# Attention on one core: the product with V in six visits instead of five, and unit 13's scores ahead of the last visit

## The chip, the cores and the metric

The kernel runs on one core of a Trainium2 chip. The metric is the device time of one execution in microseconds (us). Five engines work side by side, each through its own list of instructions: TensorE (PE; its weight loads are shown as PEld), VectorE (DVE), ScalarE (ACT), GpSimd (POOL) and SyncE (SP), which here only issues DMAs. An engine never passes over an instruction that waits for a semaphore, so what stands behind it waits too.

## What is computed

Input x is 4 sequences of 1024 tokens with 128 channels, all in float32. The reference adds an attention block and then a routed feed-forward block. Cut to what matters here:

```python
x = layernorm(layernorm(x)) * ln_w + ln_b            # 4 x 1024 x 128
q, k, v = x @ W_q + b_q, x @ W_k + b_k, x @ W_v + b_v   # 16 heads of 64
scores = q @ k.T / 8, causal mask, softmax
z = pattern @ v                                      # per head
x = resid + z @ W_o + b_o
# then: a mixture of 8 experts, 2 per token, layernorm, added to x
```

## The kernel before

Attention is done in 32 steps. A step is one pair of heads of one sequence, and has 16 **units**: unit n is query tile n // 2 (128 rows) of head n % 2, against its (n // 2 + 1) tiles of keys, so units grow from 128 to 1024 columns. Step 0, the last step and the loop body between them (30 passes on TensorE) come from one function per engine.

What a unit goes through, and under which names:

- TensorE, `scores(n)` (lines 722 and 723, full 128x128 array): two matmuls for each chunk of columns into `SPS[n % 2]`. It waits on `s_masked` until the mask of unit n - 2 has freed that buffer.
- VectorE, `mask(n)` (line 1082): masks, takes the row minimum into `NM` (a small second instruction reads it out) and writes `SSB[n % 2]`; then it signals `s_masked`.
- ScalarE, `act_exp(n)` (line 1380): the exponential into `PRS` (units 0 to 7) or `PRL` (units 8 to 15, a ring of four buffers), with the row sum.
- VectorE, `turn(n)` (line 1045): transposes the result in 32x32 blocks into `PTZ`. For even n it waits on `pv_done` until the step before has used up the key tile n // 2 there.
- TensorE, `values(...)` (lines 748 and 767): the product with V of **the step before** (`it - 1`). It runs with the array in tiles of 32 rows by 64 columns, one key tile after another; the sum over all eight is collected in the four PSUM banks `ZB`. One call is a **visit**: between visits stand scores, which use the whole array. The last two key tiles have their own order of matmuls (`last_values`) and signal once.

Behind the last visit comes the tail of the step before, `act_z` (line 1391): ScalarE copies Z out of `ZB` in two halves, banks 2 and 3 first, then 0 and 1. GpSimd's `divide` (line 532) scales by the row sums, TensorE's `out_of` (line 774) multiplies by W_o. `v_of` (line 712) projects V for the next step into banks 2 and 3 of `ZB`, so TensorE waits there for the first half of `act_z`:

```python
pe.wait_ge(z_copied, it * 2 - 1)
```

The last step has no `v_of`. After its scores TensorE also begins the next step: `scores(0, ahead=1)`, `out_of(1)`, then Q and K of the step after (line 706) between scores 1, 2, 3 and 4, and then the visit with key tile 0, which waits until unit 15 has been turned. On VectorE that turn stands directly behind `mask(2)`. The order is written out by hand in `pe_step`, `dve_step` and `act_step`; nothing schedules it at run time.

Of the kernel before, what the change touches and what calls it, by code (L numbers as in the profile page):

```python
# [55 lines left out]
def build_program(nc, a, out):  # L56
    with ExitStack() as ctx:
# [191 lines left out]
        def wait(eng, s, value):  # L249

            if not isinstance(value, int) or value > 0:
                eng.wait_ge(s, value)
# [25 lines left out]
        def spread_count(it):  # L278

            return (it + 1) * (SPREADS * DMA)  # L280

        def staged_count(it):

            return it * (3 * DMA) + 2 * DMA
# [501 lines left out]
        def pe_step(pe, it, first, last):  # L786

            step = it

            def scores(*units, ahead=0):  # L790
                it = step + ahead
                for n in units:
                    if not last and n in (UNITS // 2, UNITS // 2 + 1):

                        pe.wait_ge(qk_evac, it * 4 + n - UNITS // 2 + 7)
                    if n in (0, UNITS // 2):
                        c = n // (UNITS // 2)
                        pe.wait_ge(keys_spread[c], spread_count(it))
                        pe.wait_ge(q_split, it * 4 + 2 * c + 2)
                    wait(pe, s_masked, it * UNITS + n - 1)  # L800
                    pe_scores(pe, it, n)

            def qk(s):
                if last:
                    return
                if s == 0:
                    pe.wait_ge(staged, staged_count(it + 1))
                    if not first:
                        pe.wait_ge(x_staged[0], it * DMA)
                    pe.wait_ge(v_evac, it * 2 + 2)  # L810
                if s == 2:
                    if not first:
                        pe.wait_ge(x_staged[1], it * DMA)
                if s >= 2:

                    if first:
                        pe.wait_ge(s_masked, s - 1)
                    else:
                        pe.wait_ge(s_masked, it * UNITS + s - 3)
                pe_qk(pe, it + 1, s, ahead(s))  # L820

            def v_of(s):
                if last:
                    return
                if first:
                    pe.wait_ge(xt_ready, 6)
                else:
                    pe.wait_ge(z_copied, it * 2 - 1)
                    if s == 0:
                        pe.wait_ge(xv_staged, it * DMA)  # L830
                pe_v(pe, it + 1, s, ZB[:, 2 + s, :])

            def values(*blocks):
                if first:
                    return
                if blocks[0] == 0:
                    wait(pe, out_copied, it * 2 - 2)
                    if last:
                        pe.wait_ge(v_evac, it * 2 + 2)
                    else:  # L840
                        pe.wait_ge(qk_evac, it * 4 + 6)
                pe_values(pe, it - 1, *blocks)

            def out_of(g):
                if not first:
                    pe_out(pe, it - 1, g, TB[g])

            if first:
                scores(0, 1)
                qk(0)  # L850
                qk(1)
                scores(2)
                qk(2)
                qk(3)
                scores(3, 4)
            else:
                qk(0)
                qk(1)
                scores(1)
                qk(2)  # L860
                scores(2)
                qk(3)
                scores(3, 4)
            values(0, 1)
            scores(5, 6)
            if first:
                pe.wait_ge(qk_evac, 8)
                turn_norm(pe, 1)
            values(2)
            scores(7, 8)  # L870
            if first:
                turn_norm(pe, 2)
            values(3)
            scores(9, 10)
            if first:
                pe.wait_ge(xt_ready, 4)
                turn_norm(pe, 3)
            values(4, 5)
            scores(11, 12)
            values(6, 7)  # L880
            if first:
                pe_bias(pe)
            scores(13)
            v_of(0)
            v_of(1)
            scores(14)
            out_of(0)
            scores(15)
            if not last:
                scores(0, ahead=1)  # L890
            out_of(1)
# [230 lines left out]
        def dve_step(v, it, half, par, first, last):  # L1122

            def mask(n):
                dve_mask(v, it, par, n)

            def turn(*units):
                for n in units:
                    dve_turn(v, it, n, not first)

            def turn_back(n):
                if not first:
                    dve_turn(v, it - 1, n)

            def back():
                if not first:
                    dve_reciprocal(v, it - 1, 1 - par)

            if last:
                v.memset(BV[:, 0:P], 0.0).then_inc(zeroed, 1)  # L1140
                v.memset(ONES, 1.0).then_inc(zeroed, 1)
            if first:
                mask(0)
                mask(1)
                norm_late(v, 1)
            else:
                turn_back(13)
                mask(0)
            turn_back(14)
            if not first:  # L1150
                mask(1)
            mask(2)
            turn_back(15)
            back()
            mask(3)
            mask(4)
            if first:
                norm_late(v, 2)
            if last:
                v.wait_ge(out_evac, (STEPS - HP) * 2 + 1)  # L1160
                f_norm_stats(v, range(0, QT))
            if first:
                mask(5)
            turn(0, 1)
            if not first:
                mask(5)
            mask(6)
            turn(2, 3)
            mask(7)
            mask(8)  # L1170
            turn(4, 5)
            if last:
                f_norm_scale(v, 0)
            mask(9)
            mask(10)
            turn(6, 7, 8)
            mask(11)
            mask(12)
            if first:
                dve_bias(v)  # L1180
            turn(9, 10)
            mask(13)
            turn(11, 12)
            mask(14)
            mask(15)
# [213 lines left out]
        def act_step(act, it, half, par, first, last):  # L1399

            def exps_to(n0, n1):
                for n in range(n0, n1):
                    act_exp(act, it, par, n)

            def qk(s):
                if not last:
                    act_qk(act, it + 1, s, BQKS, ahead(s))

            def out_of(g):
                if not first:  # L1410
                    act_out(act, it - 1, g, TB[g])

            def v_of(s):
                if not last:
                    if s == 0:
                        act.wait_ge(v_stored[par], (half + 1) * DMA)
                    act_v(act, it + 1, s, ZB[:, 2 + s, :])

            if first:
                exps_to(0, 1)  # L1420
                qk(0)
                qk(1)
                exps_to(1, 2)
                qk(2)
                qk(3)
                exps_to(2, 7)
            else:
                act_exp(act, it - 1, 1 - par, UNITS - 1)
                qk(0)
                exps_to(0, 1)  # L1430
                qk(1)
                exps_to(1, 2)
                qk(2)
                qk(3)
                exps_to(2, 7)
            if first:
                norm_out(act, 1)
            if last:
                f_deviations(act, 0)
            exps_to(7, 9)  # L1440
            if first:
                norm_out(act, 2)
            exps_to(9, 11)
            if first:
                norm_out(act, 3)
            exps_to(11, 12)
            if not first:
                act_z(act, it - 1, 0)
                act_z(act, it - 1, 1)
            exps_to(12, 13)  # L1450
            v_of(0)
            exps_to(13, 14)
            v_of(1)
            out_of(0)
            exps_to(14, 15)
            out_of(1)
            if last:
                act_exp(act, it, par, UNITS - 1)
# [152 lines left out]
```

## Time and profile before

| | |
|---|---|
| median of 3 runs | 1099.04 us (1098.75 to 1099.82) |
| the profiled execution: time / span | 1098.83 us / 1097.1 us |
| PE busy, of the span | 1021.7 us, 93% |
| DVE, ACT, POOL busy | 862.3, 739.1, 740.1 us |
| instructions | 50146 |

The span runs from the first to the last instruction of one execution; its time has 1.73 us around it. "Busy" counts matmuls by modelled ends, so a TensorE that is busy 93% has few pauses, but is not at its peak rate. In the middle of the kernel every step looks like the one before it, so one step from visit to visit (500.12 us to 527.50 us) is read in detail, and the last step (from about 877 us to 909 us) beside it.

### The profile page before, as it was taken

To read this page: it belongs to the slowest core of one execution; us is meant where nothing else is said; L and a number is where in the kernel's file an instruction comes from. 1 tells how busy PE (TensorE), PEld (TensorE's weight loads), DVE (VectorE), ACT (ScalarE), POOL (GpSimd) and SP (SyncE) were. 2 spreads that over 40 slices of the span, in tenths; PEclk is the share of its full clock that TensorE was granted. 3 is DMA by queue.
4 is the path that set the end of the run, shared out by engine and by line. 5 is a ranking of instruction groups with operands and counts; after the bars stand their busy time and mean duration, and the time that the engine had idled before them with its cause. 6 is when DMAs were issued, how large, how long until landed. Compare 5 with 4: busy or idle time off the path is not lost.

```text
span 1097.1 us, 50146 instructions
## 1 busy us (share of the span) xinstructions
PE 1021.7 (93%) x19084; PEld 765.8 (70%) x19084; DVE 862.3 (79%) x2052; ACT 739.1 (67%) x1540; POOL 740.1 (67%) x725
## 2 busy tenths in 40 slices
PE   4799999999999999999999999999999988899986
PEld 2577777777777777777777777777777766454543
DVE  6878888888888888888888888888888876367574
ACT  3666666666666666666666666666666656667664
POOL 5797777777777777777777777777777734344644
PEclk8999999999999999999999999999999989999998
DMA  7678888778888788888888887888888863232422
GB/s 164 170 205 203 216 207 196 197 194 196 194 201 197 195 197 199 194 198 194 201 196 196 195 197 194 195 197 198 197 195 199 196 135 84 55 73 49 96 49 67
DMA packets 132766, 188.78 MB, mean 172 GB/s; under 512 B 46720, under 2 KB 60032, under 8 KB 132736
## 3 DMA queue, kind: packets, MB, share of 16 engines
q1 hardware_dynamic: 132736, 188.40, 71.6%
q8 instruction: 16, 0.26, 0.1%
q14 instruction: 14, 0.11, 0.0%
HBM read 133.39 MB, written 21.36 MB: 141 GB/s over the span
## 4 chain that ended last, share of the span: by engine, by line
PE 55%; DVE 27%; issue 14%; ACT 2%; DVEq 1%; DMA 1%; POOL 0%; SPq 0%; ACTq 0%
PE ZB L748 19%; DVE PTZ L1045 13%; PE SPS L722 9%; DVE SSB L1082 7%; PE SPS L723 6%; PE ZB L706 5%; PE ZB L774 3%; PE SPS L706 3%; PE SPS L939 1%; DVE NM L1082 1%; PE ZB L954 1%; PE SPS L913 1%; PE ZB L948 1%; PE ZB L931 1%; PE ZB L939 1%
## 5 line engine op out<-in xcount | busy, mean ns | idle before, releaser
L1082 DVE CUSTOM_DVE_ANT_0 SSB<-SPS,MASK 128x640 f32<-128x640 f32 (+7 forms) x512 | 375.6, 747 | 128.5 <-PE SPS L723 117.0
L722 PE MATMUL SPS<-KHP,QS 128*128 (+2 forms) x768 | 326.4, 431 | 20.1 <-DVE NM L1082 15.4
L1380 ACT ACTIVATE PRL<-SSB,NM 128x640 f32<-128x640 f32 (+3 forms) x256 | 253.4, 990 | 111.3 <-DVE NM L1082 107.7
L748 PE MATMUL ZB<-PTZ,VR 32*64 32x256 f32 (+3 forms) x12288 | 270.4, 308 | 16.0 <-DVE PTZ L1045 14.4
L748 PEld LDWEIGHTS ZB<-PTZ,VR 32*64 32x64 f32 x12288 | 229.2, 132 | 49.4 <-issue 38.3
L723 PE MATMUL SPS<-KLP,QS 128*128 (+2 forms) x768 | 261.3, 348 | 0.0
L1045 DVE STREAM_TRANSPOSE PTZ<-PRL 128x640 f32<-128x640 f32 (+3 forms) x256 | 257.7, 1027 | 0.0
L1380 ACT ACTIVATE PRS<-SSB,NM 128x128 f32<-128x128 f32 (+3 forms) x256 | 143.1, 559 | 137.6 <-DVE NM L1082 133.5
L722 PEld LDWEIGHTS SPS<-KHP,QS 128*128 128x128 f32 x768 | 145.6, 190 | 101.5 <-issue 69.7
L513 POOL TENSOR_TENSOR QS<-RAW,QS 64x512 fp32r<-64x512 f32 x128 | 165.2, 1290 | 10.3
L532 POOL TENSOR_TENSOR PTZ<-PTZ,RSB 128x512 f32<-128x512 f32 x64 | 81.1, 1288 | 133.2 <-ACT PTZ L1391 132.8
L723 PEld LDWEIGHTS SPS<-KLP,QS 128*128 128x128 f32 x768 | 145.9, 190 | 35.3 <-issue 22.6
L524 POOL TENSOR_TENSOR KLP<-RAW,KHP 64x512 fp32r<-64x512 f32 x126 | 162.1, 1286 | 10.1
L1045 DVE STREAM_TRANSPOSE PTZ<-PRS 128x128 f32<-128x128 f32 (+3 forms) x256 | 115.4, 489 | 16.9 <-PE ZB L748 16.9
L538 POOL TENSOR_TENSOR X<-X,OT 128x512 f32 (+1 forms) x64 | 81.8, 1278 | 63.6 <-ACT OT L1397 57.4
L511 POOL CAST QS<-RAW 64x512 fp32r<-64x512 f32 x128 | 77.5, 606 | 26.3 <-ACT RAW L1360 8.2
L522 POOL CAST KHP<-RAW 64x512 fp32r<-64x512 f32 x126 | 77.9, 618 | 13.2 <-POOL X L538 12.6
L774 PE MATMUL ZB<-WO,PTZ 128*128 (+1 forms) x512 | 67.4, 275 | 0.7 <-POOL PTZ L532 0.7
L774 PEld LDWEIGHTS ZB<-WO,PTZ 128*128 128x128 f32 x512 | 64.7, 191 | 4.0 <-POOL PTZ L532 1.1
L706 PE MATMUL SPS<-XTB,WQK 128*128 128x512 f32 x128 | 65.7, 598 | 0.0
L706 PE MATMUL ZB<-XTB,WQK 128*128 128x512 f32 x128 | 64.6, 630 | 0.1
L712 PE MATMUL ZB<-WV,XW 128*128 x480 | 61.1, 280 | 0.0
(178 smaller groups left out, 1209.6 us busy)
## 6 DMA issues: line engine op xcount, KB each, us to landing
VR<-v_scratch SPq DMA_DIRECT2D x248, 256.0 KB, 7.0
KHP<-KHP SPq DMA_DIRECT2D x64, 256.0 KB, 3.2
KLP<-KLP SPq DMA_DIRECT2D x64, 256.0 KB, 4.1
v_scratch<-V SPq DMA_DIRECT2D x32, 512.0 KB, 7.1
RSB<-rcp_scratch SPq DMA_DIRECT2D x64, 256.0 KB
XTB<-xt_scratch SPq DMA_DIRECT2D x62, 256.0 KB, 4.4
XW<-xt_scratch SPq DMA_DIRECT2D x30, 512.0 KB, 7.5
VR<-gate_scratch SPq DMA_DIRECT2D x16, 512.0 KB, 5.9
```

What stands on the lines that cost most here:

```text
L513: gp.tensor_tensor(QS[DH:P, h, part], q, high.bitcast(F32), ALU.subtract).then_inc(q_split, 1)
L524: gp.tensor_tensor(KL[par][DH:P, h, part], k, high.bitcast(F32), ALU.subtract).then_inc(k_split, 1)
L532: gp.tensor_tensor(z, z, RSB[:, g, :].rearrange("p (i t r) -> p i t r", t=TC, r=TR), ALU.mult).then_inc(zn_done, 1)
L538: gp.tensor_tensor(xs, xs, OT[:, :].rearrange("p (t d) -> p t d", d=D), ALU.add).then_inc(out_evac, 1)
L706: pe.matmul(bank, WQK[:, h, :], XTB[:, c * CH:(c + 1) * CH], start=True, stop=True).then_inc(qk_filled, 1)
L722: pe.matmul(SP_[n % 2][:, c0:c0 + wc], q, kh[:, c0:c0 + wc], start=True, stop=False)
L723: last = pe.matmul(SP_[n % 2][:, c0:c0 + wc], q, kl[:, c0:c0 + wc], start=False, stop=True)
L748: last = pe.matmul(ZB[h * DH:(h + 1) * DH, i, t0 * TR:QT * TR], VR[rows, j, kt, h * DH:(h + 1) * DH], turned_block(h, kt, j, rows, t0), st ...
L774: last = pe.matmul(bank[:, i * P:(i + 1) * P], ZN[g][:, i * P:(i + 1) * P], WO[:, bass.ds(it % HP, 1), :].rearrange("p o d -> p (o d)"), s ...
L1045: v.transpose(turned_of(n), exps_of(n)).then_inc(turned, 1)
L1082: v.tensor_tensor_reduce(out=SSB[n % 2][:, 0:w], in0=SP_[n % 2][:, 0:w], in1=MASK[:, S - w:S], scale=1.0, scalar=BIG, op0=ALU.add, op1=ALU ...
L1380: act.activation(exps_of(n), SSB[n % 2][:, 0:w], ACT.Exp, bias=NM[:, col:col + 1], scale=-1.0, accum_out=L[:, col:col + 1]).then_inc(exp_d ...
```

## The change

Three orders change, and nothing else: no instruction is added, removed or resized.

```diff
@@ pe_step
-            values(0, 1)
+            values(0)
             scores(5, 6)
-            values(2)
+            values(1)
             scores(7, 8)
-            values(3)
+            values(2)
             scores(9, 10)
+            values(3)
+            scores(11, 12)
             values(4, 5)
-            scores(11, 12)
-            values(6, 7)
             if first:
                 pe_bias(pe)
             scores(13)
+            values(6, 7)
             v_of(0)
             v_of(1)
@@ dve_step
-            turn(6, 7, 8)
+            turn(6, 7)
             mask(11)
             mask(12)
+            turn(8)
             turn(9, 10)
@@ act_step
-            exps_to(11, 12)
+            exps_to(11, 13)
             if not first:
                 act_z(act, it - 1, 0)
                 act_z(act, it - 1, 1)
-            exps_to(12, 13)
             v_of(0)
```

On TensorE, in the loop body, before: the end of the last visit (line 767), scores of unit 13, then `v_of` (line 712).

```order
L767 MATMUL ZB<-PTZ,VR 64x64 x2
L767 MATMUL ZB<-PTZ,VR 64x32 x24
L252 REGISTER_ALU
L722 MATMUL SPS<-KHP,QS 128x512
L723 MATMUL SPS<-KLP,QS 128x512
L722 MATMUL SPS<-KHP,QS 128x384
L723 MATMUL SPS<-KLP,QS 128x384
L828 REGISTER_ALU
L712 ISA
L712 MATMUL ZB<-WV,XW 128x128 x8
```

The same place after the change: the last of unit 13's scores, the last visit whole, then `v_of`.

```order
L723 MATMUL SPS<-KLP,QS 128x384
L767 MATMUL ZB<-PTZ,VR 64x64 x8
L767 MATMUL ZB<-PTZ,VR 64x32 x2
L767 MATMUL ZB<-PTZ,VR 64x64 x6
L767 MATMUL ZB<-PTZ,VR 64x32 x2
L767 MATMUL ZB<-PTZ,VR 64x64 x4
L767 MATMUL ZB<-PTZ,VR 64x32 x4
L767 MATMUL ZB<-PTZ,VR 64x64 x2
L767 MATMUL ZB<-PTZ,VR 64x32 x24
L828 REGISTER_ALU
L712 ISA
L712 MATMUL ZB<-WV,XW 128x128 x8
```

Nothing stands any more between the last matmul of the visit and `v_of`.

On TensorE, in the loop body, at the border of key tiles 0 and 1, before: key tile 0 ends with the 256-column matmuls, and key tile 1 (224 columns) follows at once.

```order
L748 MATMUL ZB<-PTZ,VR 64x224 x6
L748 MATMUL ZB<-PTZ,VR 64x256 x2
L748 MATMUL ZB<-PTZ,VR 64x224 x8
L748 MATMUL ZB<-PTZ,VR 64x192 x2
L748 MATMUL ZB<-PTZ,VR 64x224 x6
```

The same border after the change: the scores of units 5 and 6 stand in it.

```order
L748 MATMUL ZB<-PTZ,VR 64x224 x6
L748 MATMUL ZB<-PTZ,VR 64x256 x2
L252 REGISTER_ALU
L722 MATMUL SPS<-KHP,QS 128x384
L723 MATMUL SPS<-KLP,QS 128x384
L252 REGISTER_ALU
L722 MATMUL SPS<-KHP,QS 128x512
L723 MATMUL SPS<-KLP,QS 128x512
L748 MATMUL ZB<-PTZ,VR 64x224 x8
```

Every later pair of scores up to units 11 and 12 moves ahead of one key tile (or two) in the same way.

On ScalarE, around the copies of Z, before: exponential 11 (768 columns), the two copies, exponential 12 (896 columns).

```order
L1380 ACTIVATE PRL,L<-SSB,NM 128x768
L1390 ISA
L1391 ACTIVATE PTZ<-ZB 128x2x8x32 x2
L1377 REGISTER_ALU
L1380 ACTIVATE PRL,L<-SSB,NM 128x896
```

After the change (the same lines have numbers higher by two):

```order
L1382 ACTIVATE PRL,L<-SSB,NM 128x768
L1379 REGISTER_ALU
L1382 ACTIVATE PRL,L<-SSB,NM 128x896
L1392 ISA
L1393 ACTIVATE PTZ<-ZB 128x2x8x32 x2
```

Exponential 12 now stands ahead of the copies.

## Rows read from the trace of the kernel before

**Rows 1.** The page's chain of work that ended last, by engine

```profile
PE 55%; DVE 27%; issue 14%; ACT 2%; DVEq 1%; DMA 1%; POOL 0%; SPq 0%; ACTq 0%
```

**Rows 2.** Windows, steps 2 to 17: busy us, granted clock, DMA share, GB/s

```profile
55.00:493.00 438.00, 426.64 (x9205) 336.47 (x9206) 364.08 (x799) 303.30 (x671) 325.21 (x321) 1.00 0.82 199
```

**Rows 3.** Waits of PE, 600 to 870 us: total us, times, longest us

```profile
PE ZB L748 <- DVE PTZ L1045: 4.6, 10, 0.5
PE SPS L722 <- DVE NM L1082: 2.8, 10, 0.3
```

**Rows 4.** Timeline of PE, visits and first scores: start us, us, instruction

```profile
500.12 3.50 PE L748 MATMUL ZB<-PTZ,VR 32*64 32x256 f32 x128 [0.45 <-DVE PTZ L1045]
...
504.23 0.40 PE L723 MATMUL SPS<-KLP,QS 128*128 x1
504.56 1.56 PE L748 MATMUL ZB<-PTZ,VR 32*64 32x192 f32 x64
506.05 0.50 PE L722 MATMUL SPS<-KHP,QS 128*128 x1
506.38 0.39 PE L723 MATMUL SPS<-KLP,QS 128*128 x1
506.61 0.39 PE L722 MATMUL SPS<-KHP,QS 128*128 x1
...
507.40 1.37 PE L748 MATMUL ZB<-PTZ,VR 32*64 32x160 f32 x64
```

**Rows 5.** Timeline of PE, last visit to the next step's first visit

```profile
513.85 1.39 PE L767 MATMUL ZB<-PTZ,VR 32*64 32x64 f32 x104
515.17 0.50 PE L722 MATMUL SPS<-KHP,QS 128*128 x1
...
516.09 2.05 PE L712 MATMUL ZB<-WV,XW 128*128 x16
...
518.68 0.40 PE L723 MATMUL SPS<-KLP,QS 128*128 x1
...
520.49 0.40 PE L723 MATMUL SPS<-KLP,QS 128*128 x1
521.16 0.38 PE L722 MATMUL SPS<-KHP,QS 128*128 x1 [0.27 <-DVE NM L1082]
...
527.50 3.50 PE L748 MATMUL ZB<-PTZ,VR 32*64 32x256 f32 x128 [0.45 <-DVE PTZ L1045]
```

**Rows 6.** Timeline of DVE in the same step

```profile
506.95 0.69 DVE L1082 CUSTOM_DVE_ANT_0 SSB<-SPS,MASK 128x512 f32<-128x512 f32 x1 [0.75 <-PE SPS L723]
...
511.46 1.30 DVE L1045 STREAM_TRANSPOSE PTZ<-PRS 128x512 f32<-128x512 f32 x2
...
517.88 1.97 DVE L1045 STREAM_TRANSPOSE PTZ<-PRL 128x768 f32<-128x768 f32 x2
519.77 1.18 DVE L1082 CUSTOM_DVE_ANT_0 SSB<-SPS,MASK 128x1024 f32<-128x1024 f32 x1
520.89 0.08 DVE L1082 DVE_READ_ACCUMULATOR2_ANT NM<- 128x1 f32 x1
...
525.77 0.42 DVE L1082 CUSTOM_DVE_ANT_0 SSB<-SPS,MASK 128x256 f32<-128x256 f32 x1 [0.79 <-PE SPS L723]
526.12 1.24 DVE L1045 STREAM_TRANSPOSE PTZ<-PRL 128x1024 f32<-128x1024 f32 x1
```

**Rows 7.** Timeline of ACT: both copies of Z

```profile
515.31 1.06 ACT L1391 ACTIVATE PTZ<-ZB 128x512 f32<-128x512 f32 x2
```

**Rows 8.** Line 1391 over the kernel: ns min/median/max of one copy

```profile
L1391 ACT ACTIVATE PTZ<-ZB x64: 576/586/598, 77.2 to 928.5; 128x512 f32<-128x512 f32 x64
```

**Rows 9.** Timeline of POOL: both divisions

```profile
516.60 2.54 POOL L532 TENSOR_TENSOR PTZ<-PTZ,RSB 128x512 f32<-128x512 f32 x2 [3.87 <-ACT PTZ L1391]
```

**Rows 10.** Timeline of PE in the last step

```profile
882.88 6.36 PE L748 MATMUL ZB<-PTZ,VR 32*64 32x256 f32 x128 [0.67 <-DVE PTZ L1045]
...
905.79 1.16 PE L774 MATMUL ZB<-WO,PTZ 128*128 128x128 f32 x8 [0.70 <-POOL PTZ L532]
```

## The prediction

> **What bounds the kernel now.** I read the page first. It gives TensorE 93% of the span, but its chain of work puts 27% on VectorE [rows 1], so the two views don't name the same engine. The windows settle the shares: in the steady part TensorE is busy 426.64 of 438.00 us at a granted clock of 1.00 (the upper level, 2.4 GHz), VectorE 364.08 [rows 2]. The list of waits then tells what the remaining 2.6% is: per step TensorE pauses twice for VectorE, once for a transpose (ten times in ten steps, about 0.46 us) and once for a mask (ten times, 0.28 us) [rows 3]. The timeline of one step places them. The first visit of V begins at 500.12 and again at 527.50, so a step is 27.38 us [rows 4, 5]. One pause is before that visit; the other, at 521.16, is before `scores(0, ahead=1)` and ends with the mask of unit 14 (its minimum is read out by 520.97, TensorE goes on 0.19 later) [rows 5, 6]. There are no other pauses. So TensorE paces the step, VectorE catches it at two points, and a new order can gain at most those two pauses and must not open a third.
>
> Counted from start to start, the pause at 521.16 is larger than its 0.27: full chunks of scores follow each other by 0.23 (506.38 to 506.61) [rows 4], so after the one at 520.49 the next was due at 520.72 and came 0.44 late [rows 5].
>
> **The change, part by part.** All matmuls, masks, exponentials, transposes, copies and DMAs stay, in number and size. What can change is the price of switching between scores and visits, and who waits.
>
> *A sixth visit.* Key tile 2 alone takes 1.56 us and key tile 3 alone 1.37 [rows 4], 0.19 less for one tile of queries less. Continued upwards, key tiles 1 and 0 alone would take 1.75 and 1.94, together 3.69, against 3.50 in one visit [rows 4]. Each visit's last matmuls overlap the scores behind it by 0.07 (504.56 + 1.56 = 506.12, next start 506.05) [rows 4], so the split adds 3.69 - 3.50 - 0.07 = 0.12. The way in costs 0.10: from the last scores (504.23) to the visit (504.56) it is 0.33 where scores follow by 0.23. The way out costs 0.10 as well: 506.05 to 506.38 is 0.33 [rows 4]. The new sixth way out is the one from the last visit into `v_of`, behind the new wait, and its 0.10 is the price of weights loaded uncovered; the scores at 521.16, which now would not come out of a pause, save about the same (an estimate from the same 0.10). I let these two cancel. Visits: **+0.22 us a step**, bounds 0 (the extrapolation fails, and the way in hides) and 0.35.
>
> The Trainium skill, TensorEngine Tiling (Array Packing), Key Properties, says that changing the tiling mode makes the array drain. Visits and scores are in two such modes, and the change makes ten mode changes a step into twelve. The 0.33 against 0.23 agrees with it; were the rule without effect here, the time would come out about 7 us lower than mine.
>
> *The last visit directly ahead of `v_of`.* Today the last visit ends at 513.85 + 1.39 = 515.24 and ScalarE starts the copies 0.07 later, at 515.31; the first is done after 0.59, at 515.90, and `v_of` starts at 516.09 [rows 5, 7, 8]. In between TensorE does the scores of unit 13 (515.17 to 516.09, 0.92). They hide the copy almost exactly. After the change that cover is gone. `v_of` could start 0.07 before the visit's modelled end; instead it starts 0.07 + 0.59 + 0.14 to 0.19 behind it (0.14 is from the end of the transpose at 526.12 + 1.24 = 527.36 to 527.50, 0.19 the mask's release above) [rows 5, 6]. That is 0.87 to 0.92: **+0.89 us a step**. The bound from below is 0.70, if the second half's distance (1.06 - 0.59 = 0.47) is what a copy costs and ScalarE starts at once [rows 7]; the bound from above is 1.0. Behind the wait stand `v_of`, scores 14, `out_of(0)` and scores 15. Exponential 12 is ahead of the copies now, but it must not be late: VectorE's masks 11 and 12 come out earlier (below), and even with turn 8, whose buffer of the ring it needs, behind mask 12, it is over well before the visit's end. Leaving it behind the copies would have been harmless too.
>
> *Masks earlier.* The new starts on TensorE, with the pieces above (1.87 and 1.68 for key tiles 0 and 1 up to the next start, all other distances as today): scores 5 at 501.99, 7 at 504.68, 9 at 507.52, key tile 3 at 509.10 to 510.47, scores 11 at 510.40, scores 13 at 513.97, last visit 514.99 to 516.38. Scores 5 to 13 reach VectorE 1.2 to 1.8 us sooner. Transposes are held by key tiles instead: turn 6 needs key tile 3, free at 510.47, so about 510.6 instead of 511.46. From there to the end of turn 12 VectorE has the same instructions and today no pause, ending at 519.77 [rows 6]; so it is done at about 518.9. TensorE meanwhile is later by 0.22 + 0.89 (+0.10) = 1.21 from `v_of` on: scores 14 end at 519.08 + 1.21 = 520.29, and VectorE waits for them.
>
> *The pause for mask 14.* It arises today since mask 14 starts at 519.77, behind turn 12, though scores 14 end at 518.68 + 0.40 = 519.08 [rows 5, 6]. A free VectorE starts 0.17 after the scores (506.38 + 0.39 = 506.77, 506.95) [rows 4, 6]: at 519.25 in today's times. Mask and readout take 1.20 (519.77 to 520.97), the release 0.19: 520.64, and TensorE is due at 520.72. So the pause goes, with 0.08 to spare: **-0.44 us a step**; bounds -0.44 and 0.
>
> *The pause for turn 15.* Mask 2 starts as soon as scores 2 are there (VectorE idles 0.79 before it), turn 15 follows at 526.12 and the visit 0.14 behind its end [rows 5, 6]. All of it hangs on TensorE's own scores 2 and moves with them. Mask 15 is now released by scores 15 rather than by mask 14: VectorE gets later against TensorE by about 0.43 of the 0.79, and another 0.10 goes where scores 0 come out uncovered no more. 0.26 is left, so this pause stays as it is: 0.
>
> *Others.* The divisions start 0.23 after the copies' end (516.37 to 516.60) and take 1.27 each [rows 9]; new: about 517.7 to 519.0, and `out_of(0)` comes at about 520.1. Covered by 1.1 us. SyncE's spread of V waits for key tile 3, later by 1.7 us, and for the last visit; both feed a visit 15 us or more later. GpSimd's splits and its adds shift with the step.
>
> **The sum.** 0.22 + 0.89 - 0.44 = +0.67 us for each of the 30 steps with a `v_of` behind a visit, 20.1 us. The last step has no `v_of`, but its `out_of(0)` already waits 0.70 for GpSimd [rows 10], so the whole chain visit, copies, division shows: the visit ends later by 0.22 and by the scores 13 now ahead of it (0.92 + 0.10), about 1.2 us. Step 0 has no visits. Together +21.3 on the profiled execution's 1098.83 (1.73 around its span; the median of runs, 1099.04, is 0.02% off): **1120 us**, 1.9% slower. 0.2% is about what a measurement of this kernel can tell from no change, and this is far above it.
>
> **Rivals.**
> - *The mask 14 pause stays* (0.08 is little): something makes VectorE 0.5 late, say a turn held longer by a key tile. Then +1.11 a step, 33 + 1.2: 1133 us.
> - *Switching is free, or the copy's release shorter.* Without the 0.22 and with 0.75 for the wait: +0.31 a step: 1109 us.
> - *VectorE paces the step* (other side). For it: the 27%, and both pauses end there [rows 1, 3]. Then the earlier masks are worth their whole effect, the copy of Z falls into a time in which TensorE would wait anyway, and the step gains 0.44 - 0.22: 31 steps, -7 us: 1092 us. It decides once the wait before `v_of` is under 0.22 us. Against it: the copy alone takes 0.58 at least in all 64 cases [rows 8], and at that point TensorE has no pause today that could take it in.
> - *The clock falls.* In the last step, behind several pauses of TensorE, the first visit took 6.36 us instead of 3.50 [rows 4, 10]: the lower level, 1.2 GHz. Were each step's new pause to do that to one visit, 2.9 us a step would be added: about 1207 us. The Trainium skill, TensorE: Matmul & The Clock Gate, Part 1, has the clock fall after an idle engine; by it a longer pause would count. Against it: two pauses a step today, at a clock of 1.00 [rows 2, 3].
>
> **Chances.** The forecast with its bounds 0.78, the pause that stays 0.09, the cheap case 0.06, VectorE as the pace 0.03 (faster), the clock 0.02, and 0.02 for a balance near nothing. The range 1109 to 1134 takes in the first three. Faster by over 0.2%: 0.04; within: 0.03; slower: 0.93.
>
> **What would show it.** A new pause of some 0.8 us in every step, TensorE line 712 waiting for ScalarE's copy of Z, 30 times; no or nearly no wait of scores for a mask; the transpose pause still about 0.46; six visits, of about 1.94 and 1.75 us for the first two; steps of 28.05 us. VectorE's idle time should sit before mask 14 and before the turns of units 2, 4 and 6. I am wrong if the copy is released much faster than other hand-overs, if the pause at mask 14 survives, or if the visits' length hides stalls that the new order removes, which the modelled ends can't show.

## The result and the profile after

| | before | after |
|---|---|---|
| median of 4 runs each, same chip, us | 1099.23 (1098.75 to 1099.82) | 1121.27 (1120.95 to 1123.54) |
| ratio to before | | 1.0206 [1.0194, 1.0219] |
| profiled execution: time, span, us | 1098.83, 1097.1 | 1123.54, 1121.5 |
| granted clock in steps 2 to 17 | 1.00 [rows 2] | 1.00 |
| one step, first visit to first visit, us | 27.38 [rows 4, 5] | 28.09 |

The change costs 22.0 us, 2.1%; 1120 was predicted. The profiled execution of after is the longest of its four. In step 2 one of its visits waits 2.0 us for the spread of V, a wait that the trace of before doesn't have; whether the other three executions had it isn't known. The comparisons below go by a step of the steady part, which this doesn't touch.

The page of after: the span, the busy time of the engines, and the chain of work that ended last.

```profile
span 1121.5 us, 50146 instructions
...
PE 1026.5 (92%) x19084; PEld 758.9 (68%) x19084; DVE 869.7 (78%) x2052; ACT 741.3 (66%) x1540; POOL 740.1 (66%) x725
...
PE 79%; DVE 9%; ACT 4%; issue 3%; DMA 3%; SPq 1%; POOL 0%; DVEq 0%; POOLq 0%; ACTq 0%
```

The number of instructions is the same. VectorE's share of the chain fell from 27% [rows 1] to 9% and TensorE's rose from 55% to 79%, while the kernel became slower: a share of the chain tells whom the end is traced through, not what the step costs.

The waits of TensorE in the trace of after, from 600 to 880 us (total us, times, longest us).

```profile
PE ZB L712 <- ACT PTZ L1393: 8.3, 10, 0.8
PE ZB L748 <- DVE PTZ L1046: 4.6, 10, 0.5
```

Against [rows 3], the waits of scores for a mask are gone, the transpose pause stands as it was, and a new and larger wait has come: `v_of` for ScalarE's copy of Z, once a step. The same list over the whole kernel:

```profile
PE ZB L712 <- ACT PTZ L1393: 25.0, 30, 0.8
PE ZB L748 <- DVE PTZ L1046: 14.0, 30, 0.7
...
PE SPS L722 <- DVE NM L1083: 6.9, 8, 2.3
...
PE ZB L748 <- DMA VR<-v_scratch: 2.0, 1, 2.0
```

The new wait comes 30 times and sums to 25.0 us, more than the whole loss; before, the waits for a mask were 36 and 15.4 us over the whole kernel, so 28 of them and 8.5 us have gone. The last row is the wait in step 2. Now one step of TensorE after (start us, duration us), the answer to [rows 4, 5].

```profile
512.97 1.99 PE L748 MATMUL ZB<-PTZ,VR 32*64 32x256 f32 x64 [0.45 <-DVE PTZ L1046]
514.89 0.44 PE L722 MATMUL SPS<-KHP,QS 128*128 x1
...
515.57 0.40 PE L723 MATMUL SPS<-KLP,QS 128*128 x1
515.90 1.77 PE L748 MATMUL ZB<-PTZ,VR 32*64 32x224 f32 x64
517.60 0.50 PE L722 MATMUL SPS<-KHP,QS 128*128 x1
...
527.92 1.39 PE L767 MATMUL ZB<-PTZ,VR 32*64 32x64 f32 x104
530.14 2.05 PE L712 MATMUL ZB<-WV,XW 128*128 x16 [0.83 <-ACT PTZ L1393]
531.95 0.48 PE L722 MATMUL SPS<-KHP,QS 128*128 x1
...
534.77 0.34 PE L722 MATMUL SPS<-KHP,QS 128*128 x1
...
541.06 1.99 PE L748 MATMUL ZB<-PTZ,VR 32*64 32x256 f32 x64 [0.46 <-DVE PTZ L1046]
```

The reader is to see three things. Key tiles 0 and 1 are visits of 1.99 and 1.77 us with scores between. Behind the last visit TensorE stands for 0.83 us until `v_of` at 530.14. And from `v_of` to the next first visit it is 10.92 us, against 11.41 before (516.09 to 527.50 [rows 5]): there the mask's pause is missing. The other side of the new wait is ScalarE:

```profile
527.46 1.04 ACT L1382 ACTIVATE PRL<-SSB,NM 128x896 f32<-128x896 f32 x1 [0.80 <-DVE PTZ L1046]
...
529.35 1.08 ACT L1393 ACTIVATE PTZ<-ZB 128x512 f32<-128x512 f32 x2 [0.75 <-PE ZB L767]
```

Exponential 12 is over before the copies, with ScalarE idle for 0.75 us in between. The first copy starts 0.04 us behind the visit's modelled end (527.92 + 1.39 = 529.31), and takes 0.59. And VectorE in the same step:

```profile
515.01 0.51 DVE L1046 STREAM_TRANSPOSE PTZ<-PRS 128x128 f32<-128x128 f32 x2 [0.35 <-PE ZB L748]
...
517.72 0.77 DVE L1046 STREAM_TRANSPOSE PTZ<-PRS 128x256 f32<-128x256 f32 x2 [0.86 <-PE ZB L748]
...
520.56 1.04 DVE L1046 STREAM_TRANSPOSE PTZ<-PRS 128x384 f32<-128x384 f32 x2 [0.52 <-PE ZB L748]
...
529.86 1.97 DVE L1046 STREAM_TRANSPOSE PTZ<-PRL 128x768 f32<-128x768 f32 x2
533.30 1.22 DVE L1083 CUSTOM_DVE_ANT_0 SSB<-SPS,MASK 128x1024 f32<-128x1024 f32 x1 [1.47 <-PE SPS L723]
534.45 0.08 DVE L1083 DVE_READ_ACCUMULATOR2_ANT NM<- 128x1 f32 x1
...
539.34 0.42 DVE L1083 CUSTOM_DVE_ANT_0 SSB<-SPS,MASK 128x256 f32<-128x256 f32 x1 [0.43 <-PE SPS L723]
539.69 1.24 DVE L1046 STREAM_TRANSPOSE PTZ<-PRL 128x1024 f32<-128x1024 f32 x1
```

Mask 14 (533.30) now waits 1.47 us for its scores, where in [rows 6] it started late, behind a transpose. The transposes wait for key tiles instead, and 0.43 us is left ahead of mask 2 (0.79 before [rows 6]).

### The profile page after: what moved, and what is told of

Its sections match the earlier page's. It is cut to its first block, busy times and chain, and to the rows that moved or that the text cites. A ratio compares the mean times of both kernels' runs of the same rounds, so it can differ in the third digit from the quotient of the medians.

```text
span 1121.5 us, 50146 instructions
## 1 busy us (share of the span) xinstructions
PE 1026.5 (92%) x19084; PEld 758.9 (68%) x19084; DVE 869.7 (78%) x2052; ACT 741.3 (66%) x1540; POOL 740.1 (66%) x725
## 4 chain that ended last, share of the span: by engine, by line
PE 79%; DVE 9%; ACT 4%; issue 3%; DMA 3%; SPq 1%; POOL 0%; DVEq 0%; POOLq 0%; ACTq 0%
PE ZB L748 23%; PE SPS L722 14%; PE SPS L723 11%; PE ZB L712 5%; PE ZB L774 5%; PE ZB L706 5%; PE ZB L767 4%; DVE PTZ L1046 3%; PE SPS L706 2%; ACT PTZ L1393 2%; PE SPS L940 1%; PE ZB L955 1%; PE SPS L914 1%; PE ZB L949 1%; PE ZB L932 1%
## 5 line engine op out<-in xcount | busy, mean ns | idle before, releaser
L748 PE MATMUL ZB<-PTZ,VR 32*64 32x256 f32 (+3 forms) x12288 | 277.3, 307 | 16.3 <-DVE PTZ L1046 14.0
L748 PEld LDWEIGHTS ZB<-PTZ,VR 32*64 32x64 f32 x12288 | 220.9, 131 | 58.0 <-issue 45.0
L712 PEld LDWEIGHTS ZB<-WV,XW 128*128 128x128 f32 x480 | 55.8, 191 | 28.2 <-issue 28.2
```

The costliest lines, as they stand in the source:

```text
L712: last = pe.matmul(bank[:, k * P:(k + 1) * P], xt[:, t * P:(t + 1) * P], WV[:, bass.ds((it % HP) * 2, 2), :].rearrange("p h e -> p (h e)") ...
L748: last = pe.matmul(ZB[h * DH:(h + 1) * DH, i, t0 * TR:QT * TR], VR[rows, j, kt, h * DH:(h + 1) * DH], turned_block(h, kt, j, rows, t0), st ...
```

## The experiments

The theory is that of the prediction: the step grows by a wait of some 0.8 us that the copy of Z opens ahead of `v_of`, and by switching (a sixth visit), less the pause for mask 14. The rivals were that VectorE's or ScalarE's new order is what costs, and that the visits rather than the wait carry the loss. "Step" is always the time between two first visits in the steady part. All the kernels compute the whole reference.

### Cover for the copy: scores 13 back behind the last visit

```diff
-            scores(13)
             values(6, 7)
+            scores(13)
             v_of(0)
```

> The changed kernel with one part undone: scores 13 stand behind the last visit again, so 0.92 us of matmuls lie between the visit and v_of. Six visits, masks, exponentials and transposes as in the change. Theory (the loss is the bare wait of v_of for the copy of Z, 0.90 us a step, plus 0.30 for the sixth visit, less 0.49 for the pause of mask 14): the wait before v_of falls to 0.1 us or less, the pause of mask 14 stays away or returns with less than 0.15, a step takes 27.2 to 27.4 us, the kernel 1095 to 1100 us. Rival (the loss sits in VectorE's new order, its turns held back by key tiles): the step stays above 27.9 us, the kernel above 1112 us.

Measured: 1095.42 us, ratio 0.9974 [0.9957, 0.9992]; a step is 27.20 us (524.95 to 552.15). The timeline of TensorE:

```profile
537.00 1.85 PE L748 MATMUL ZB<-PTZ,VR 32*64 32x128 f32 x126
...
538.70 1.35 PE L767 MATMUL ZB<-PTZ,VR 32*64 32x64 f32 x100
539.98 0.50 PE L722 MATMUL SPS<-KHP,QS 128*128 x1
```

The wait is 0.19 us a step instead of 0.83, and the kernel that was 2.1% slower is now 0.3% faster than before. The expectation had an error: with scores 13 gone from between them, key tiles (4, 5) and (6, 7) run as one visit. It takes 2.98 us (537.00 to 539.98), so there are five visits and not six, and this run takes away the wait and one switch together. It can't size the wait alone; the next one does.

### Cover for the copy: scores 14 ahead of v_of, six visits kept

```diff
             values(6, 7)
+            scores(14)
             v_of(0)
             v_of(1)
-            scores(14)
             out_of(0)
```

> The changed kernel with scores 14 moved between the last visit and v_of; scores 13 stay ahead of the visit. Theory: about 0.98 us of matmuls cover the copy of Z, the wait of v_of falls below 0.1 us, the pause of mask 14 stays away since its scores are even earlier, a step takes 27.1 to 27.3 us, the kernel 1092 to 1097 us. Rival (scores this early only queue up on VectorE, or out_of of the first half, which now comes right behind v_of, waits for GpSimd's divisions): a new wait on TensorE of 0.3 us or more a step, the kernel at 1101 to 1112 us.

Measured: 1099.27 us (12 runs, 1095.47 to 1103.06), ratio 1.0009 [0.9991, 1.0026]; a step is 27.29 us (526.75 to 554.04). The timeline of TensorE:

```profile
541.68 1.39 PE L767 MATMUL ZB<-PTZ,VR 32*64 32x64 f32 x104
543.00 0.50 PE L722 MATMUL SPS<-KHP,QS 128*128 x1
543.34 0.40 PE L723 MATMUL SPS<-KLP,QS 128*128 x1
...
544.04 1.95 PE L712 MATMUL ZB<-WV,XW 128*128 x16
545.89 1.15 PE L774 MATMUL ZB<-WO,PTZ 128*128 x8
```

`v_of` starts without a wait behind the moved scores, and the mask's pause doesn't come back. Against after, one pair of matmul groups has changed places and the step is 0.80 us shorter; 30 steps make 24 us, and 22.0 were measured. So the uncovered copy is the loss. The step gets back 0.80 and not the whole 0.90 of the wait because the way out of the last visit shows again: the second matmul of scores 14 comes 0.34 behind the first, where scores otherwise follow by 0.23. With the copy covered, the rest of the change gains nothing that can be measured against the kernel before: what the masks give, the sixth visit takes.

The median did miss the expected 1092 to 1097: the profiled execution, the shortest of twelve, is in it, while the others are up to 7.6 us longer. The five above 1100 us had a mean granted clock of 0.980 to 0.982, six of the other seven one of 0.985 or more. Where in the kernel they lost it isn't known, since only one execution was traced.

### The split alone, in the kernel before

```diff
-            values(0, 1)
-            scores(5, 6)
+            values(0)
+            scores(5)
+            values(1)
+            scores(6)
```

> The kernel before with one edit: key tiles 0 and 1 in two visits, scores 5 between them and scores 6 behind the second; all else as before. Theory (each further visit costs TensorE about 0.30 us, by 3.76 against 3.50 us for the visits, 0.07 overlap, 0.10 for the way in): 31 steps of +0.30, 1108 to 1109.5 us, pauses as before. Rival (the switch costs nothing in itself, only its waits do): 1099 to 1101 us.

Measured: 1110.54 us, ratio 1.0103 [1.0078, 1.0128]; a step is 27.75 us (507.17 to 534.92), 0.37 more. TensorE's timeline (line numbers are higher by one here):

```profile
534.92 1.99 PE L748 MATMUL ZB<-PTZ,VR 32*64 32x256 f32 x64 [0.46 <-DVE PTZ L1047]
...
537.39 1.77 PE L748 MATMUL ZB<-PTZ,VR 32*64 32x224 f32 x64
```

Both pauses of before are still there (0.46 and 0.27 us a step), so the 0.37 is the price of the further visit and not of a wait: 1.99 + 1.77 - 3.50 = 0.26, less 0.07 of overlap, and 0.10 each for the way in and the way out make 0.39. Over 31 steps 0.37 is 11.5 us; 11.3 were measured. The expectation of 0.30 a step, and with it 1109.5 us at most, was too low, since it had left out the way out. One more visit in a step costs 1% of this kernel. The Trainium skill, TensorEngine Tiling (Array Packing), Key Properties, says that the array drains when the tiling mode changes. The 0.10 on either side agrees with that. How much of the 0.26 inside the visits is the same drain isn't shown, since no run splits a visit without changing the mode.

### The copy in three pieces

The changed kernel with `act_z` called for bank 2, bank 3 and banks 0 and 1, so that each `v_of` waits for one bank only.

```diff
-            banks = slice(2 - k * 2, 4 - k * 2)
+            banks = (slice(2, 3), slice(3, 4), slice(0, 2))[k]
...
-                    pe.wait_ge(z_copied, it * 2 - 1)
+                    pe.wait_ge(z_copied, it * 3 - 2 + s)
```

> The changed kernel with the copy of Z in three pieces instead of two (bank 2, bank 3, banks 0 and 1), so that the first half of v_of waits for 256 columns only. Theory (TensorE's wait is the copy's own length plus the hand-over): a piece takes about 0.37 us instead of 0.59, the pause before v_of falls from 0.83 to 0.6 us, the kernel to 1113 to 1116 us. Rival (the wait is a hand-over whose length has nothing to do with the copy): 1120 to 1122 us.

Measured: 1114.49 us, ratio 1.0136 [1.0109, 1.0162]; a step is 27.88 us. The same place of the timeline of TensorE, and the copies over the kernel (ns, min/median/max):

```profile
524.57 2.05 PE L712 MATMUL ZB<-WV,XW 128*128 x16 [0.62 <-ACT PTZ L1393]
```

```profile
L1393 ACT ACTIVATE PTZ<-ZB x96: 378/384/606, 78.0 to 944.8; 128x256 f32<-128x256 f32 x64, 128x512 f32<-128x512 f32 x32
```

A first piece of 0.38 instead of 0.59 us takes 0.21 off the wait, and the step is 0.21 shorter: 6.3 us over 30 steps, with 6.8 measured against the changed kernel. The wait follows the copy's duration one for one.

### ScalarE's part undone

```diff
-            exps_to(11, 13)
+            exps_to(11, 12)
             if not first:
                 act_z(act, it - 1, 0)
                 act_z(act, it - 1, 1)
+            exps_to(12, 13)
```

> The changed kernel with ScalarE's order undone: exponential 12 behind both copies of Z again. Theory (the position of exponential 12 is off the path: the copies start at the visit's end either way, and turn 12 is needed only before mask 14, which now waits for its scores): 1120 to 1123 us, the pause before v_of unchanged at 0.83 us. Rival (exponential 12 behind the copies delays turn 12 and mask 14, as the change's order suggests): the pause before scores 0 comes back with 0.2 us or more a step, 1126 us or more.

Measured: 1120.94 us, ratio 1.0194 [1.0171, 1.0217]; the step is 28.08 us, and the wait before `v_of` still 0.83. ScalarE idles 2.67 us ahead of the copies instead of 0.75:

```profile
526.72 1.08 ACT L1393 ACTIVATE PTZ<-ZB 128x512 f32<-128x512 f32 x2 [2.67 <-PE ZB L767]
```

The copy starts when the visit ends, wherever exponential 12 stands. This part of the change makes no difference that could be measured.

### VectorE's part undone

```diff
-            turn(6, 7)
+            turn(6, 7, 8)
             mask(11)
             mask(12)
-            turn(8)
```

> The changed kernel with VectorE's order undone: turn 8 ahead of mask 11 again. Turn 8 needs key tile 4, which TensorE now uses up only behind scores 12. Theory: VectorE stands about 1.5 us before turn 8, mask 11 comes late, scores 13 wait for it about 1.1 us a step: 1150 to 1160 us. Rival (VectorE's idle time of 1.47 us before mask 14 takes it in): 1120 to 1125 us.

Measured: 1153.95 us, ratio 1.0487 [1.0462, 1.0511]; a step is 29.23 us, 1.14 more than after. VectorE and TensorE in one step:

```profile
512.12 0.84 DVE L1046 STREAM_TRANSPOSE PTZ<-PRL 128x640 f32<-128x640 f32 x1 [1.53 <-PE ZB L748]
```

```profile
513.87 0.50 PE L722 MATMUL SPS<-KHP,QS 128*128 x1 [1.07 <-DVE NM L1083]
```

Turn 8 has to wait for key tile 4, now visited behind scores 11 and 12. Mask 11 is queued behind it, and scores 13 wait 1.07 us for that mask. So VectorE's part of the change is needed by TensorE's part. The loss of after doesn't come from it: the waits of scores for a mask have gone from the list there.

### Five visits and three pieces together

The first and the fourth edit joined.

> Scores 13 behind the last visit again and the copy of Z in three pieces: six visits without the wait. Theory: of the 0.19 us that v_of still waited with scores 13 behind, nothing is left; 27.0 us a step, 1087 to 1092 us. Rival (the sum of TensorE's order is not what remains; VectorE's chain from mask 13 to mask 14 sets the step now): the step stays at 27.2 us and a pause for a mask comes back, 1094 to 1097 us.

Measured: 1090.19 us, ratio 0.9909 [0.9890, 0.9927]; a step is 27.03 us. These are five visits again and not the six of the expectation, as in the first experiment. The list of TensorE's waits from 600 to 860 us is one line:

```profile
PE ZB L748 <- DVE PTZ L1046: 4.6, 10, 0.5
```

```profile
537.27 0.34 PE L723 MATMUL SPS<-KLP,QS 128*128 x1
537.58 2.05 PE L712 MATMUL ZB<-WV,XW 128*128 x16
```

The wait of `v_of` is no longer listed, but a rest of it is there: it starts 0.31 us behind the last matmul of scores 13, against 0.17 (515.92 to 516.09) in the trace of before. A wait shorter than the modelled length of the matmul ahead of it doesn't show in the list (537.27 + 0.34 = 537.61 lies behind 537.58). Without the sixth visit and with the copy nearly covered, what the change did for the masks remains, and the kernel is 0.9% faster than before.

### The remaining pause: turn 15 ahead of mask 2

Three kernels, all starting from the last one (scores 13 behind, three pieces). The first has two edits: turn 15 ahead of mask 2 on VectorE, and one unit of scores on TensorE moved behind `values(0)`:

```diff
@@ pe_step
-                scores(3, 4)
+                scores(3)
             values(0)
+            if not first:
+                scores(4)
             scores(5, 6)
@@ dve_step
-            mask(2)
             turn_back(15)
+            mask(2)
```

> As the one with scores 13 behind and three pieces, and the pause before the first visit attacked: on VectorE turn 15 ahead of mask 2, on TensorE scores 4 behind key tile 0. Theory (that pause is there only because turn 15 stands behind mask 2, which waits for TensorE's scores 2): the pause falls from 0.46 to 0.1 us or less, a step takes 26.6 to 26.7 us, 1075 to 1082 us. Rival (exponential 15 or the chain of VectorE is the later one): the pause stays above 0.3 us, 1087 us or more.

Measured: 1099.95 us, ratio 1.0003 [0.9986, 1.0019]; a step is 27.36 us (499.85 to 527.21), 0.33 more than without the two edits: a clear miss. The first visit doesn't wait any more, but the time is back, and more, at scores 6:

```profile
527.21 1.98 PE L748 MATMUL ZB<-PTZ,VR 32*64 32x256 f32 x64
...
530.54 0.50 PE L722 MATMUL SPS<-KHP,QS 128*128 x1 [0.43 <-DVE NM L1085]
```

Three units of scores (4, 5 and 6) stand in one gap, and the third needs the buffer of the first, which is free only after the mask of unit 4; that mask can't begin before TensorE has finished scores 4 in this same gap. The second kernel therefore keeps VectorE's exchange alone:

> Scores 13 behind and three pieces, and on VectorE alone turn 15 ahead of mask 2; TensorE's order untouched. Theory (the pause before the first visit is closed by a chain that ends at scores 4 as well, since they wait for mask 2): the transpose pause goes, a pause for mask 2 of about 0.4 us takes its place before scores 4, step 26.95 to 27.1 us, 1088 to 1092 us. Rival (turn 15 alone closed it): 26.6 us a step, 1078 us.

Measured: 1087.35 us, ratio 0.9886 [0.9852, 0.9919]; a step is 26.93 us, 0.10 shorter. The expectation had the place right and the pause too long, so the time is just below its range. The pause moved from the visit to scores 4 ahead of it, and shrank from 0.46 to 0.15:

```profile
547.38 0.44 PE L722 MATMUL SPS<-KHP,QS 128*128 x1 [0.15 <-DVE NM L1083]
```

That the step gains only 0.10 and not 0.31 shows when starts are compared. Scores 4 come 0.31 late (0.43 behind the matmul before them, where 0.12 is usual) and their second matmul another 0.11 (0.28 behind the first instead of 0.17). The visit came 0.53 late in the kernel of the last section (0.80 behind the last scores, where it is 0.27 here). 0.53 less 0.42 is 0.11.

The third moves the units from 4 on by one, in all steps but step 0, so that no gap has three: behind key tile 0 stand scores 4 and 5, behind 1 scores 6 and 7, and so on to 10 and 11 behind key tile 3 and scores 12 between the last two visits. VectorE's order is moved to match, and exponential 12 stands behind the copies again.

```diff
             values(0)
-            scores(5, 6)
+            scores(4, 5)
             values(1)
-            scores(7, 8)
+            scores(6, 7)
...
             values(3)
-            scores(11, 12)
+            scores(10, 11)
             values(4, 5)
+            scores(12)
             values(6, 7)
             scores(13)
```

> Turn 15 first, and all scores from unit 4 on moved one visit on (0; 4, 5; 1; 6, 7; 2; 8, 9; 3; 10, 11; 4 and 5; 12; 6 and 7; 13), with VectorE's order to match, so that no pair of scores needs the mask of the pair before it in the same gap. Theory (TensorE's order is the step: no pause left, one visit more than with scores 13 behind, for 0.37 us): about 26.9 us a step, 1082 to 1089 us. Rival (VectorE, whose turns and masks now alternate with TensorE's visits, opens a new pause of 0.3 us or more): 1092 us or more.

Measured: 1085.24 us (6 runs, 1082.22 to 1092.55), ratio 0.9864 [0.9830, 0.9898]; a step is 26.83 us (520.81 to 547.64), and from 600 to 860 us TensorE has no wait in its list. The intervals of these last two overlap, so which is the better isn't settled; by their medians they are 1.1% and 1.4% faster than the kernel before. With no wait listed, a step is nearly matmuls and switching only (scores 0 still come 0.11 late, 541.84 to 542.18), and six visits instead of five (27.03 less 0.46 would be 26.57, measured 26.83) take back part of what the last pause gave.

The profiled execution is the longest of the six, 1092.55 us, and its clock differs from that of all other traces (us, busy us and instructions of each engine, granted clock, DMA share, GB/s):

```profile
60.00:380.00 320.00, 319.90 (x6885) 249.28 (x6886) 269.31 (x587) 217.59 (x503) 239.51 (x237) 0.95 0.83 201
```

TensorE is busy without a pause, and the granted clock is 0.95 until about 390 us and 1.00 from 400 to 860 us. A step in the slower stretch takes 27.17 us (223.43 to 250.60) and not the 26.83 read above at 1.00, which over 12 steps makes about 4 us, an estimate. Over the whole kernel this execution has a mean clock of 0.960, the other five 0.982 to 0.985. Why it was lower once in six isn't known.

## Why the prediction was right

The steady step went as predicted, 28.09 us measured against 28.05, and by the mechanism that was named. That it is only 0.04 off is in part luck: the further visit cost about 0.07 more than forecast, and the pause for mask 14 gave back 0.05 more.

- **The wait before `v_of`, +0.89 predicted.** Measured: the last visit could hand over at 527.92 + 1.39 - 0.07 = 529.24, and `v_of` starts at 530.14: +0.90. It is made as the prediction made it: start of the copy 0.04 behind the visit (0.07 was taken), 0.59 of copy, 0.20 to TensorE. Shown by taking it away (0.80 us less a step with scores 14 as cover, the way out of the visit being back) and by shortening it (0.21 for 0.21).
- **The sixth visit, +0.22 predicted: the term that was most off.** The visits took 1.99 and 1.77, not 1.94 and 1.75: together 0.26 above the joint visit, where the extrapolation gave 0.19. With -0.07 and the 0.10 of the way in it is +0.29. The step downwards from 1.56 to 1.37 was 0.19; upwards it is 0.21 and 0.22. I had taken it as constant.
- **The pause for mask 14, -0.44 predicted.** From `v_of` to the next first visit it is 0.49 less. The pause itself accounts for 0.44. The other 0.05 is in scores 0, whose first matmul sits 0.17 in front of the next, against 0.22 before. VectorE was free in time: it stood 1.47 us ahead of mask 14, so the rival of 1133 us, with VectorE 0.5 late, had no ground. Behind the mask the margin was as narrow as forecast. The minimum is read out by 534.45 + 0.08 = 534.53, and with a release of 0.19 scores 0 could start at 534.72; they start at 534.77, at their usual distance. About 0.05 was to spare where 0.08 was forecast.
- **The way out into `v_of`, let cancel against scores 0.** From `v_of` to scores 14 it is 1.81 us both times (530.14 to 531.95; in the trace of before 516.09 to 517.90, there behind scores), so nothing of a mode change shows inside it. I read this as the cost lying under the wait, since TensorE stands there anyway; the run with scores 14 as cover, where the 0.10 comes back, agrees. So both halves were mis-sized: 0 and not +0.10 for the way out, -0.05 and not -0.10 for scores 0. Their sum is -0.05 and not 0. That the 0.10 is the price of weights loaded uncovered, as the prediction says, no run shows.
- **The transpose pause, unchanged.** 0.46, as predicted. 0.43 of idle time is left ahead of mask 2, where the prediction had 0.26.
- **`out_of(0)` and the clock.** `out_of(0)` starts at 532.96 without a wait; the predicted 520.1, moved by the 12.85 between the two profiled steps, is 532.95. The granted clock is 1.00, the upper level, with two pauses of 0.83 and 0.46 a step. The Trainium skill, TensorE: Matmul & The Clock Gate, Part 1, has the clock fall after an idle engine. Idle times of this size don't do it in the steady steps. It did fall in the last step of the trace of before, at about 881.9, after TensorE had stood 0.94 and 0.85 us close together, ahead of scores 2 and 3.
- **The last step, +1.2 predicted.** From its first visit to the matmuls of the end it is 27.97 us (906.22 to 934.19) against 26.77 (882.88 to 909.65): +1.20. The total was right by accident, since the clock did two things that the sum left out, and they cancel.

```profile
906.22 3.49 PE L748 MATMUL ZB<-PTZ,VR 32*64 32x256 f32 x64 [0.74 <-DVE PTZ L1046]
...
910.79 1.77 PE L748 MATMUL ZB<-PTZ,VR 32*64 32x224 f32 x64
...
928.95 2.07 PE L774 MATMUL ZB<-WO,PTZ 128*128 128x128 f32 x8 [1.21 <-POOL PTZ L532]
...
934.19 0.49 PE L981 MATMUL SPS<-XW,BV 128*128 128x128 f32 x2
```

The windows from `out_of` to the matmuls of the end, before and after (the granted clock is the third number from the end):

```profile
905.00:909.70 4.70, 3.12 (x22) 2.67 (x21) 4.70 (x9) 3.25 (x8) 3.26 (x3) 1.00 0.54 133
```

```profile
928.90:934.20 5.30, 5.25 (x21) 4.70 (x21) 1.54 (x5) 1.72 (x3) 2.49 (x2) 0.53 0.76 170
```

Up to the first `out_of` the step is not longer at all, 22.73 us (906.22 to 928.95) against 22.91 (882.88 to 905.79). Before, the granted clock is at its lower level (1.2 GHz) for about 7 us there and the first visit takes 6.36 instead of 3.50; after, it is for about 3.5 us, and the first visit takes 3.49 instead of 1.99. That is 1.36 us less lost to the clock. Without it the part would be 1.18 longer, which is the forecast chain of visit, copies and division (an estimate from these durations). Behind it the clock takes about as much back: from `out_of` to the end it is 5.24 us against 3.86, at a granted clock of 0.53 instead of 1.00 (the 0.88 us that TensorE waited there before for a mask lie under the slower matmuls now). It fell at about 927.0, after TensorE had stood 1.41 us in the last visit (up to 925.76). Why the first low stretch was shorter isn't shown.

Together 30 x 0.71 + 1.2 = 22.5 us, and the medians differ by 22.0. In most of the experiments the measured difference is likewise up to three microseconds off 30 times that of the step; the start of the kernel and the last step weren't followed closely enough to say where that is.

## What to carry to other kernels

An order that puts a producer directly ahead of the consumer of its evacuation pays release, copy and release in full (here 0.9 us a step), however idle the copying engine is; before work is pulled forward from between the two, look what it was covering, and leave other work in its place (here scores 13 left 0.19 us of the wait, and scores 14 none). Where a matrix engine switches between two tiling modes, count the switches as one counts instructions: here one further visit cost 0.37 us, most of the 0.49 that the earlier masks gave. And where two buffers take turns, a third unit in one gap waits for the mask of the first, so that a pause removed ahead of the gap is back inside it.

## What was not expected of the hardware

- A change of tiling mode that fell behind a wait cost nothing more here: the way out of the last visit, 0.10 us elsewhere, is not seen at `v_of` when TensorE stands 0.83 us first.
- Two visits that lie next to each other run as one. Key tiles (4, 5) and (6, 7) take 2.98 us together, and 3.18 apart (525.04 to 526.90 is 1.86, and 513.85 to 515.17 in [rows 5] is 1.32), the ways in and out of the second one not counted.
- Half the columns take 65% of the time in ScalarE's copy out of PSUM: 0.38 us for 256, 0.59 for 512. Splitting it shortens what a consumer waits for by less than half.
- One visit waited for the spread of V in five of the twelve profiled kernels: 2.0 us in after and in the split alone, 0.6 to 1.4 us in three others, and not at all in the kernel before. In what share of their executions that happens wasn't tried.
- The granted clock was 0.95 for over 300 us in the profiled execution of the one kernel in which TensorE never paused, and 1.00 in the same stretch of all other traces.
